# Another order of work at the turn from attention to the feed-forward part of a transformer block

## The chip, the cores and the metric

The kernel runs on one core of one Trainium2 chip. The metric is the device time of one execution, in microseconds (us). The kernel before takes 2203.07 us, the median of three executions between 2202.29 and 2204.08.

A core has five engines that work side by side, each through its own list of instructions: TensorE (PE in the profile; its weight loads are PEld), VectorE (DVE), ScalarE (ACT), GpSimd (POOL) and SyncE (SP), which here only issues DMA transfers. They wait for each other through semaphores. SBUF is the on-chip memory, PSUM the small memory into which TensorE writes sums.

## The reference

One block of a transformer on an input x of 8 batches, 512 rows and 512 columns, in float32:

```python
x = x + attention(layernorm(x))      # 16 heads, low-rank queries and keys
x = x + ffn(layernorm(x))            # 512 -> 1536 -> 512, weights rounded to fp8
layernorm(x) = (x - mean) / sqrt(var + 1e-5)
ffn(n) = (silu((n @ gate) * gs) * ((n @ up) * us)) @ down * ds
```

The change lies in the second layernorm: after the last head of a batch has been added to x, its rows are normalised, and the result is what gate and up are multiplied with.

## The kernel before, in words

The batches 0 to 7 go one after the other. Within a batch the 512 rows are four tiles of 128 rows, one row to a partition. The 16 heads of attention come first, then the feed-forward part in 12 chunks of 128 columns. Every product on TensorE is made in float16 with operands cut in two: a high half (the value rounded to float16) and a low half (what the rounding left), so that three products, or two where the weight is exact, give nearly the float32 result.

**The turn** is the stretch between the last head of a batch and the first gate products. For batches 1 to 6 it is done so:

- `add_out` (line 1956, VectorE) adds the last head to the residual rows `XR`, tile by tile, and leaves the sum of every row in `row_sum`. ScalarE follows one tile behind with `squares` (line 1496): the sum of squared deviations of each row, in `row_sq`. What it writes beside that, into `XN2`, is not used.
- VectorE makes 1/sqrt(variance) by a chain of nine small steps, each of which waits for the one before (`rsqrt`, lines 1724 to 1760; `RSQRT_OPS` is 9). Before, there are two chains: one for the tiles 0 and 1, as soon as their squares are there, and one for the tiles 2 and 3. Between the chains stands `layer_norm` (line 1788), which writes (x - mean) / deviation as float32 into `XN2` for tiles 0 and 1, and after the second chain the same for tiles 2 and 3.
- ScalarE rounds the high halves from `XN2` (`x_rows_hi`, line 1339), VectorE makes the low halves from `XN2` and the high ones (`x_rows_lo`, through `split_lo`, line 1694). The low halves of tiles 0 and 1 are put between the steps of the second chain. The high ones are in `XHL[:, 0]`, the low ones in `XHL[:, 1]`.
- SyncE issues four transposing DMAs (`turn_rows`, line 547), always in this order: high halves of tiles 0 and 1, low halves of tiles 0 and 1, high halves of 2 and 3, low halves of 2 and 3. Each waits for its two tiles. They turn rows into columns, as TensorE needs them, and end in `XTT`.
- TensorE has other work meanwhile: the last head's output, and the latent products of the next batch (`latent` in the tensor block), which end with the k latents of tile 3. Then comes `turned_gates` (lines 1156 to 1170, products at line 1142): 64 products of 128x256 for the first two chunks. The first 16 wait for the first transpose, the next 16 for the second, the next 12 for the third, the last 20 for the fourth.
- ScalarE has also the latents of the next batch to read out of PSUM (`latent`, lines 1350 and 1352), before, between and after the high halves. Its order before is: squares, latent 3, high halves 0 and 1, latents 4 and 5, high halves 2 and 3, latents 6 and 7.

All of these orders are written out by hand; nothing is planned by a scheduler. Batch 0 has a turn of its own, in which TensorE transposes the rows and one chain of nine steps serves all four tiles; batch 7 has another. The diff leaves the order of both as it is.

Of the kernel before, what the change touches and what calls it, by code (L numbers as in the profile page):

```python
# [20 lines left out]
F32 = mybir.dt.float32  # L21
# [4 lines left out]
ALU = mybir.AluOpType  # L26
ACT = mybir.ActivationFunctionType
AX_X = mybir.AxisListType.X

P = 128  # L30
B, S, H = 8, 512, 512
# [5 lines left out]
NT = S // P  # L37
# [4 lines left out]
EPS_LN = 1e-5  # L42
# [3 lines left out]
XS = 2.0**6  # L46
# [61 lines left out]
def build(nc, x, w_a, w_pe, w_nope, w_k, w_v, w_o, norm_cols, kv_norm_row, w_ffn,  # L108
# [3 lines left out]
    with ctx:  # L112
        def sb(name, shape, dt):
            return ctx.enter_context(nc.sbuf_tensor(name, shape, dt))
# [32 lines left out]
        rden_end = sb("rden_end", [P, NT], F32)  # L147
        row_sum = sb("row_sum", [P, NT], F32)
        row_sq = sb("row_sq", [P, NT], F32)


        ARENA_B = 109056
# [158 lines left out]
        def any_bank(n):  # L311
# [5 lines left out]
            "stored", "turn", "c_cols", "k_scaled", "ab_psum", "vo_psum", "w_hi", "w_lo", "ab_cp", "ab_hi", "ab_lo",  # L317
            "f_a", "f_aw", "f_b", "f_bw", "f_clip", "f_diff", "f_free",
            "ln_chain", "set_chain", "rms_chain", "k_chain",
            "ln1_chain", "x32", "xs", "xt1", "xn", "xtp", "xth", "xtl", "qkv", "ssq",  # L320
            "kvh", "kvl", "qsh", "qsl", "kt_t", "kr", "kph", "kpl",
            "qpp", "rot4", "rot", "qpeh", "qpel",
            "lat", "qap", "qah", "qal", "mxr", "shift",
# [954 lines left out]
        def _(act):  # L1278
# [55 lines left out]
            def x_rows_hi(b, t):  # L1334

                if t == 0:
                    act.wait_ge(s["ctp"], (b + 1) * N_CT)
                act.wait_ge(s["xn"], (b + 1) * NT + t + 1)
                act.activation(XHL[:, 0, t, :], XN2[:, t, :], ACT.Copy, scale=XS).then_inc(s["xth"], 1)

            def latent(a, i, setup=False):

                which, t = latents_order(setup)[i]
                n, raw = (QL, QN[:, t, :]) if which == "q" else (KL, KRAW[:, t, :])
                src = latent_banks(setup, a)[which][t]
                act.wait_ge(s["qkv"], a * (2 * NT) + (i + 1))
                if not (setup and i == 0):
                    act.wait_ge(s["ssq"], a * (2 * NT) + i)
                col = 0 if which == "q" else 1
                act.activation(JUNK[:, 0:n], src[:, 0:n], ACT.Square, scale=float(PROJ / np.sqrt(n)),  # L1350
                               accum_out=ss[:, t, col:col + 1]).then_inc(s["ssq"], 1)
                act.activation(raw, src[:, 0:QL if which == "q" else KL + DR], ACT.Copy).then_inc(s["lat"], 1)
# [156 lines left out]
            def attention(b, last, first, plain):  # L1509
                base = b * NH  # L1510
                if not first:
                    act.wait_ge(s["yo"], b * NT)
                if not plain:
                    act.wait_ge(s["t_out"], 16 * N_DUO)
                if plain:
                    probs(base, 0, True)
                    qa_hi(base + 2, 0)
                    rot_hi(b, rot_first(b))
                else:
                    probs_divided(b, 0)  # L1520
                if first:
                    rot_hi(b, N_ROT - 2)
                    probs(base + 1, 1, False)
                    rot_hi(b, N_ROT - 1)
                elif plain:
                    probs(base + 1, 1, False)
                    for n in range(rot_first(b) + 1, N_ROT):
                        rot_hi(b, n)
                else:
                    probs_divided(b, 1)  # L1530
                qa_hi(base + 3, 1)
                if not plain:
                    rot_hi(b, N_ROT_FFN)
                if first:
                    round_half(0)
                    round_rest(0)
                    for i in range(2, NH - 2):
                        head_step(i, base, i % 2, chunk=chunk_of(i), weights=True)
                elif plain:
                    for i in range(2, NH - 2):  # L1540
                        head_step(i, base, i % 2)
                        if i >= 4 and i % 2 == 0:
                            sum_hi(i // 2 - 2)
                        for t in ROWS_PLAIN.get(i, ()):
                            next_rows_hi(b, t)
                else:
                    for i in range(2, NH - 2):
                        probs_divided(b, i)
                        qa_hi(base + i + 2, i % 2)
                        if i in STG_STEPS and not last:  # L1550
                            next_rows_hi(b, STG_STEPS.index(i))
                for k in range(2):
                    i = NH - 2 + k
                    if first and k == 0:
                        output_hi(i)
                    if plain:
                        probs(base + i, k, False)
                    else:
                        probs(base + i, k, False, halves_landed(b, i), (b, i - 2))
                    if first and k == 0:  # L1560
                        output_hi(NH - 1)
                        round_half(chunk_of(i))
                        round_rest(chunk_of(i))
                    if plain and not first and k == 0:
                        sum_hi(N_DUO - 2)
                    if not last:
                        latent(b + 1, k)
                if first:
                    round_half(chunk_of(NH - 1))
                    round_rest(chunk_of(NH - 1))  # L1570
                elif plain:
                    sum_hi(N_DUO - 1)
                if last:
                    made = order_of_duo(b, N_DUO - 1)
                    context_half_hi(b, 0)
                    context_half_hi(b, 1)
                    squares(b, 0, made + 6)
                    squares(b, 1, made + 7)
                    x_hi(b + 1, (0, 1))
                    squares(b, 2, made + 11)  # L1580
                    squares(b, 3, made + 12)
                    x_hi(b + 1, (2, 3))
                    return
                latent(b + 1, 2)
                if not plain:
                    context_half_hi(b, 0, VBANK_LATE, NH - 1)
                    context_half_hi(b, 1, VBANK_LATE, NH - 1)
                for t in range(NT):
                    squares(b, t, (b * NH + NH - 1) * NT + t + 1)
                if first:  # L1590
                    for i in range(3, 2 * NT - 2):
                        latent(b + 1, i)
                    x_hi(b + 1, (0, 1))
                    latent(b + 1, 2 * NT - 2)
                    x_hi(b + 1, (2, 3))
                    latent(b + 1, 2 * NT - 1)
                    return
                latent(b + 1, 3)
                x_rows_hi(b, 0)
                x_rows_hi(b, 1)  # L1600
                latent(b + 1, 4)
                latent(b + 1, 5)
                x_rows_hi(b, 2)
                x_rows_hi(b, 3)
                latent(b + 1, 6)
                latent(b + 1, 7)

# [84 lines left out]
        def _(dve):  # L1692
# [28 lines left out]
                dve.wait_ge(s["f_clip"], c + 1)  # L1721
                dve.tensor_tensor(f_clip, f_b16[k], f_clip, ALU.subtract).then_inc(s["f_diff"], 1)

            def rsqrt(ch, v, n, eps, ops=range(RSQRT_OPS), at=0, out=None, scale=1.0, of=None, within=None):

                ve, y, t, u = rs_v[:, at:at + n], rs_y[:, at:at + n], rs_t[:, at:at + n], rs_u[:, at:at + n]
                as_v = (lambda a: a.rearrange("p (a b) -> p a b", a=v.shape[1])) if len(v.shape) == 3 else lambda a: a
# [1 line left out]

                def link(ins):  # L1730
                    ch.add(ins)
                    if within is not None and k in within:
                        within[k]()
                    ch.wait()

                for k in ops:
                    if k == 0 and of is not None:
# [23 lines left out]

            LN_N = 9 + RSQRT_OPS
            LN2_N = 1 + RSQRT_OPS
            LN3_N = 1 + 2 * RSQRT_OPS

            def norms_done(b):
                return LN_N if isinstance(b, int) and b == 0 else LN_N + LN2_N + (b - 1) * LN3_N

            assert LN_N == 18

# [25 lines left out]

            def x_rows_lo(b, t):

                dve.wait_ge(s["xth"], (b + 1) * NT + t + 1)
                split_lo(XHL[:, 1, t, :], XN2[:, t, :], XS, XHL[:, 0, t, :]).then_inc(s["xtl"], 1)  # L1800

            LN1_N = 9 + RSQRT_OPS

# [372 lines left out]
            def last_of_attention(b, first):  # L2176
# [57 lines left out]
                if first:  # L2234
# [5 lines left out]
                    layer_norm(XN2, XR)  # L2240
                    x_lo(u)
                    return
                lo, hi = row_sq[:, 0:2], row_sq[:, 2:4]
                dve.wait_ge(s["sq"], b * NT + 2)
                rsqrt(ch, lo, 2, EPS_LN, range(0, 1), of=1.0 / H ** 3)
                means()
                rsqrt(ch, lo, 2, EPS_LN, range(1, RSQRT_OPS), of=1.0 / H ** 3)
                layer_norm(XN2, XR, (0, 1))
                dve.wait_ge(s["sq"], b * NT + NT)
                rsqrt(ch, hi, 2, EPS_LN, at=2, of=1.0 / H ** 3,  # L2250
                      within={1: lambda: x_rows_lo(b, 0), 3: lambda: x_rows_lo(b, 1)})
                assert ch.n == LN3_N
                layer_norm(XN2, XR, (2, 3))
                x_rows_lo(b, 2)
                x_rows_lo(b, 3)

            def ffn(b, last, first):
                def tile_step(c):
# [399 lines left out]
```

## Time and profile before

| | |
|---|---|
| median of three executions | 2203.07 us |
| the profiled execution | 2201.61 us |
| its span | 2199.8 us |
| TensorE busy | 2170.0 us (99%) |
| VectorE busy | 1575.5 us (72%) |
| ScalarE busy | 1306.4 us (59%) |
| GpSimd busy | 1361.5 us (62%) |
| granted TensorE clock | 1.0 of full speed |

The profile is of one execution. Times in its rows are microseconds from the start of its span; a batch takes about 266 us of it. "x2" behind a row means that two instructions of one kind were joined in it; the time is then from the first one's start to the last one's end. What stands in square brackets is how long the engine sat idle before the row, and who ended that.

### The profile page before, as it was taken

The page shows a single profiled execution, that of the slowest core. Times are in us where ns is not written, and L with a number is a line of the kernel's source. Part 1 is how long each engine was busy: PE and PEld are TensorE (multiplying, and loading weights), DVE is VectorE, ACT ScalarE, POOL GpSimd, SP SyncE. Part 2 cuts the span into 40 slices and gives each one's busy share as a digit, 9 for nine tenths or more (in the row PEclk, how much of TensorE's full clock was granted, in tenths as well). Part 3 has the DMA queues.
Part 4 walks back from the last instruction along what each step waited for, and adds up shares of the span by engine and source line. Part 5 has one row for each costly group of instructions (what it writes and reads, how often), then busy time and mean ns, then how long its engine had stood idle before and what let it go on. Part 6 is the DMA issues. An engine that isn't in the chain of part 4 may idle for free.

```text
span 2199.8 us, 37599 instructions
## 1 busy us (share of the span) xinstructions
PE 2170.0 (99%) x11728; PEld 1099.1 (50%) x11728; DVE 1575.5 (72%) x3593; ACT 1306.4 (59%) x2764; POOL 1361.5 (62%) x1083
## 2 busy tenths in 40 slices
PE   7999999999999999999999999999999999999999
PEld 5444544445445564455644555445554556445554
DVE  7888786877677775777667776577766777467773
ACT  6666664555377742876428754487534875367732
POOL 4656465785378733987249772588535884368742
PEclk9999999999999999999999999999999999999999
DMA  7868436766168940788408873198632996248740
GB/s 246 192 122 149 100 72 151 154 139 151 30 127 161 167 116 19 158 161 166 99 27 164 164 152 84 46 167 159 138 80 64 165 170 125 48 99 157 152 82 20
DMA packets 759721, 271.86 MB, mean 124 GB/s; under 512 B 712656, under 2 KB 729040, under 8 KB 758480
## 3 DMA queue, kind: packets, MB, share of 16 engines
q1 hardware_dynamic: 759504, 269.35, 59.6%
q8 instruction: 90, 1.47, 0.3%
q14 instruction: 127, 1.04, 0.1%
HBM read 79.31 MB, written 14.81 MB: 43 GB/s over the span
## 4 chain that ended last, share of the span: by engine, by line
PE 89%; DVE 5%; DMA 2%; ACT 1%; POOL 1%; issue 1%; SPq 0%; ACTq 0%; DVEq 0%; POOLq 0%
PE bank L1180 12%; PE bank L961 9%; PE scores L1190 7%; PE bank L359 7%; PE bank L361 7%; PE bank L360 7%; PE scores L847 5%; PE scores L361 5%; PE scores L360 5%; PE scores L359 5%; PE bank L866 4%; PE bank L868 4%; PE bank L867 4%; PE scores L844 3%; DMA arena<-arena 2%; PE bank L1142 2%
## 5 line engine op out<-in xcount | busy, mean ns | idle before, releaser
L1926 DVE TENSOR_REDUCE mx<-scores 128x1 f32<-128x512 f32 x512 | 353.2, 690 | 61.1 <-PE scores L361 60.8
L2471 POOL TENSOR_TENSOR arena<-arena 128x1024 f16<-128x1024 f32 x168 | 354.4, 2131 | 37.0 <-ACT arena L1448 37.0
L1432 ACT ACTIVATE arena<-scores,shift 128x512 f32<-128x512 f32 x336 | 229.3, 686 | 146.8 <-DVE shift L1928 101.7
L1180 PE MATMUL bank<-arena,WFF 128*128 128x512 f16 x1296 | 292.8, 379 | 0.8 <-DVE arena L2262 0.6
L2011 DVE SCALAR_TENSOR_TENSOR arena<-bank,arena 128x512 f32<-128x512 f32 x336 | 217.0, 686 | 75.9 <-PE bank L961 74.6
L2572 POOL TENSOR_TENSOR arena<-arena 128x512 f16<-128x512 f32 x96 | 115.1, 1199 | 251.2 <-ACT arena L1618 251.2
L2384 POOL TENSOR_TENSOR arena<-arena 128x1024 f16<-128x1024 f32 x88 | 187.8, 2138 | 94.1 <-ACT arena L1422 93.6
L961 PE MATMUL bank<-WVO 128*128 128x256 f16 x1764 | 213.6, 273 | 0.2 <-DVE arena L2011 0.2
L1180 PEld LDWEIGHTS bank<-arena,WFF 128*128 128x128 f16 x1296 | 126.6, 98 | 152.8 <-DVE arena L2262 2.3
L847 PE MATMUL scores<-arena 128*128 128x512 f16 x512 | 195.4, 382 | 0.0
L961 PEld LDWEIGHTS bank<-WVO 128*128 128x128 f16 x1764 | 172.1, 98 | 46.1 <-DVE arena L2011 1.4
L359 PE MATMUL scores<-arena 128*128 128x512 f16 x512 | 194.0, 379 | 0.0
L360 PE MATMUL scores<-arena 128*128 128x512 f16 x512 | 194.0, 379 | 0.0
L361 PE MATMUL scores<-arena 128*128 128x512 f16 x512 | 194.0, 379 | 0.0
L1420 ACT ACTIVATE arena<-scores,shift 128x512 f32<-128x512 f32 x176 | 122.4, 696 | 119.6 <-DVE shift L1928 113.9
L1612 ACT ACTIVATE arena<-bank,gsc 128x512 f32<-128x512 f32 x96 | 65.6, 683 | 203.5 <-PE bank L1180 168.4
L866 PE MATMUL bank<-arena 128*128 128x512 f16 x476 | 180.4, 379 | 1.3 <-DMA arena<-arena 1.0
L868 PE MATMUL bank<-arena 128*128 128x512 f16 x476 | 180.4, 379 | 0.0
L867 PE MATMUL bank<-arena 128*128 128x512 f16 x476 | 180.4, 379 | 0.0
L1190 PE MATMUL scores<-WFF,arena 128*128 128x512 f16 x736 | 173.9, 379 | 0.0
L2459 POOL TENSOR_TENSOR arena<-arena,rden_duo 128x512 f32<-128x512 f32 x102 | 108.0, 1066 | 102.2 <-DVE rden_duo L1969 102.2
L1446 ACT ACTIVATE arena<-arena,rden_duo 128x512 f16<-128x512 f32 x234 | 166.7, 712 | 0.0
(206 smaller groups left out, 4727.8 us busy)
## 6 DMA issues: line engine op xcount, KB each, us to landing
WVO<-w_duo SPq DMA_DIRECT2D x42, 512.0 KB, 4.5
WVO<-w_duo SPq DMA_DIRECT2D x42, 384.0 KB, 3.9
arena<-arena SPq DMA_TRANSPOSE x736, 3.3
arena<-w_ffn SPq DMA_DIRECT2D x24, 384.0 KB, 3.5
arena<-x SPq DMA_DIRECT2D x8, 1024.0 KB, 5.7
out<-arena SPq DMA_DIRECT2D x32, 256.0 KB, 2.1
arena<-x SPq DMA_DIRECT2D x14, 512.0 KB, 5.8
WVO<-w_o SPq DMA_DIRECT2D x4, 1024.0 KB, 8.2
```

The source lines that it names most:

```text
L359: pe.matmul(dst, lhsT=ls(0), rhs=rs(0), start=first, stop=False)
L360: pe.matmul(dst, lhsT=ls(0), rhs=rs(1), start=False, stop=False)
L361: return pe.matmul(dst, lhsT=ls(1), rhs=rs(0), start=False, stop=last)
L847: pe.matmul(dst, lhsT=Q1[:, par, tile(t)], rhs=KA[:, :], start=False, stop=False)
L866: pe.matmul(dst[:, :], lhsT=KV[:, 0, j, :], rhs=PT[:, par, 0, :, j, :], start=(j == 0), stop=False)
L867: pe.matmul(dst[:, :], lhsT=KV[:, 1, j, :], rhs=PT[:, par, 0, :, j, :], start=False, stop=False)
L868: m = pe.matmul(dst[:, :], lhsT=KV[:, 0, j, :], rhs=PT[:, par, 1, :, j, :], start=False, stop=(j == NT - 1))
L961: r = pe.matmul(dst, lhsT=XP[j % 2][:, p, x, tile(t)], rhs=WB[:, q, w, :], start=(start and t == 0 and m == 0), stop=(m == 2), skip_group_ ...
L1180: m = pe.matmul(dst[:, :], lhsT=w[:, c, k, :], rhs=rows(p, k), start=(k == 0 and p == 0), stop=(k == NK - 1 and p == 1))
L1190: m = pe.matmul(SC[:, t, :], lhsT=FU[:, c % 4, p, tile(t)], rhs=WD[:, c, :], start=(c == 0 and p == 0), stop=(c == NF - 1 and p == 1))
L1926: dve.tensor_reduce(mx[:, t:t + 1], SC[:, t, :], AX_X, ALU.max).then_inc(s["mxr"], 1)
L2471: pool.tensor_tensor(PL[:, par, two, :], exps(i)[:, two, :], PH[:, par, two, :], ALU.subtract).then_inc(s["pl"], 1)
```

## The change

In batches 1 to 6 one chain of nine steps serves all four tiles. It starts when all four tiles have their squares. Its result carries the scale XS = 64 that the halves have. A new small instruction on VectorE makes `rs_n` = -mean times that root, with a semaphore `nb` of its own. ScalarE no longer reads `XN2`: it makes a high half from `XR` in one activation, root times x plus `rs_n`, as soon as `nb` is raised. VectorE then makes `XN2` for all four tiles and after that the four low halves. On ScalarE latent 5 moves behind the high halves of tiles 2 and 3. SyncE's and TensorE's lists stay as they are.

```diff
+        rs_n = sb("rs_n", [P, NT], F32)
...
@@ x_rows_hi (ScalarE)
-                act.wait_ge(s["xn"], (b + 1) * NT + t + 1)
-                act.activation(XHL[:, 0, t, :], XN2[:, t, :], ACT.Copy, scale=XS).then_inc(s["xth"], 1)
+                act.wait_ge(s["nb"], b)
+                act.activation(XHL[:, 0, t, :], XR[:, t, :], ACT.Identity, scale=rs_y[:, t:t + 1],
+                               bias=rs_n[:, t:t + 1]).then_inc(s["xth"], 1)
@@ attention (ScalarE)
                 x_rows_hi(b, 0)
                 x_rows_hi(b, 1)
                 latent(b + 1, 4)
-                latent(b + 1, 5)
                 x_rows_hi(b, 2)
                 x_rows_hi(b, 3)
+                latent(b + 1, 5)
                 latent(b + 1, 6)
                 latent(b + 1, 7)
@@ x_rows_lo (VectorE)
+                dve.wait_ge(s["xn"], (b + 1) * NT + t + 1)
                 dve.wait_ge(s["xth"], (b + 1) * NT + t + 1)
-                split_lo(XHL[:, 1, t, :], XN2[:, t, :], XS, XHL[:, 0, t, :]).then_inc(s["xtl"], 1)
+                split_lo(XHL[:, 1, t, :], XN2[:, t, :], 1.0, XHL[:, 0, t, :]).then_inc(s["xtl"], 1)
@@ last_of_attention (VectorE)
-                lo, hi = row_sq[:, 0:2], row_sq[:, 2:4]
-                dve.wait_ge(s["sq"], b * NT + 2)
-                rsqrt(ch, lo, 2, EPS_LN, range(0, 1), of=1.0 / H ** 3)
                 means()
-                rsqrt(ch, lo, 2, EPS_LN, range(1, RSQRT_OPS), of=1.0 / H ** 3)
-                layer_norm(XN2, XR, (0, 1))
                 dve.wait_ge(s["sq"], b * NT + NT)
-                rsqrt(ch, hi, 2, EPS_LN, at=2, of=1.0 / H ** 3,
-                      within={1: lambda: x_rows_lo(b, 0), 3: lambda: x_rows_lo(b, 1)})
-                assert ch.n == LN3_N
-                layer_norm(XN2, XR, (2, 3))
-                x_rows_lo(b, 2)
-                x_rows_lo(b, 3)
+                ch.wait()
+                rsqrt(ch, row_sq[:], NT, EPS_LN, scale=XS, of=1.0 / H ** 3)
+                dve.scalar_tensor_tensor(out=rs_n[:], in0=mv[:, :, 0], scalar=-1.0, in1=rs_y[:, 0:NT], op0=ALU.mult,
+                                         op1=ALU.mult).then_inc(s["nb"], 1)
+                assert ch.n == LN2_N
+                layer_norm(XN2, XR)
+                for t in range(NT):
+                    x_rows_lo(b, t)
```

The rest of the diff is bookkeeping: the count of chain steps per batch in `norms_done`, the semaphore's name, and the way in which `rsqrt` writes down the value it waits for, which is the same value for every chain that is left.

## Rows read from the trace of the kernel before

**Rows 1.** Page, part 1: busy us (share of the span) x instructions.
```profile
PE 2170.0 (99%) x11728; PEld 1099.1 (50%) x11728; DVE 1575.5 (72%) x3593; ACT 1306.4 (59%) x2764; POOL 1361.5 (62%) x1083
```

**Rows 2.** Timeline, gate products of batches 1, 2, 3, 4, 5, 6: start, us, engine, line.
```profile
536.35 7.29 PE L1142 MATMUL bank<-arena,WFF 128*128 128x256 f16 x64 [0.16 <-DMA arena<-arena]
801.64 7.44 PE L1142 MATMUL bank<-arena,WFF 128*128 128x256 f16 x64
1067.29 3.65 PE L1142 MATMUL bank<-arena,WFF 128*128 128x256 f16 x32 [0.19 <-DMA arena<-arena]
1071.70 3.67 PE L1142 MATMUL bank<-arena,WFF 128*128 128x256 f16 x32 [0.76 <-DMA arena<-arena]
1337.58 3.67 PE L1142 MATMUL bank<-arena,WFF 128*128 128x256 f16 x32 [0.36 <-DMA arena<-arena]
1604.95 3.67 PE L1142 MATMUL bank<-arena,WFF 128*128 128x256 f16 x32 [1.57 <-DMA arena<-arena]
1867.08 7.21 PE L1142 MATMUL bank<-arena,WFF 128*128 128x256 f16 x64 [0.16 <-DMA arena<-arena]
```

**Rows 3.** Timeline of batch 3's turn: VectorE and ScalarE.
```profile
1060.23 0.16 DVE L1738 TENSOR_SCALAR rs_v<-row_sq 128x2 f32<-128x2 f32 x1
1061.14 0.18 ACT L1496 ACTIVATION_READ_ACCUMULATOR arena<-arena,row_sum 128x1 f32 x1
1062.08 1.00 DVE L1788 TENSOR_SCALAR arena<-arena,mv,rs_y 128x512 f32<-128x512 f32 x2
1062.66 1.15 ACT L1339 ACTIVATE arena<-arena 128x512 f16<-128x512 f32 x2 [0.44 <-DVE arena L1788]
1063.72 0.47 ACT L1350 ACTIVATE arena<-scores 128x384 f16<-128x384 f32 x1
1064.55 0.28 ACT L1350 ACTIVATE arena<-scores 128x128 f16<-128x128 f32 x1
1066.35 1.15 ACT L1339 ACTIVATE arena<-arena 128x512 f16<-128x512 f32 x2 [1.21 <-DVE arena L1788]
1067.02 1.29 DVE L1694 SCALAR_TENSOR_TENSOR arena<-arena 128x512 f16<-128x512 f32 x2 [0.24 <-ACT arena L1339]
1068.49 0.34 ACT L1352 ACTIVATE arena<-scores 128x192 f32<-128x192 f32 x1
```

**Rows 4.** Timeline of batch 0's turn, VectorE: one chain for four tiles.
```profile
257.96 0.17 DVE L1738 TENSOR_SCALAR rs_v<-row_sq 128x4 f32<-128x4 f32 x1 [0.83 <-ACT arena L1496]
259.75 1.92 DVE L1788 TENSOR_SCALAR arena<-arena,mv,rs_y 128x512 f32<-128x512 f32 x4
```

**Rows 5.** Timeline, transposes of batch 3 as SyncE issues them (x4 from first, x3 from second).
```profile
1063.91 7.01 SPq L547 DMA_TRANSPOSE arena<-arena  x4
1065.27 5.65 SPq L547 DMA_TRANSPOSE arena<-arena  x3
```

**Rows 6.** Chain of waits, third transpose in batches 2, 3, 4, 5: issued, us to landing.
```profile
802.15 3.22 DMA arena<-arena
1067.60 4.06 DMA arena<-arena
1333.89 3.65 DMA arena<-arena
1599.97 4.93 DMA arena<-arena
```

**Rows 7.** DMA queues between 1067.6 and 1072 us: packets, MB, share of 16 engines.
```profile
q1 hardware_dynamic: 2089, 0.52, 91.6%
q8 instruction: 1, 0.02, 2.0%
```

**Rows 8.** Groups of ScalarE: busy us, mean ns of one, idle before.
```profile
L1446 ACT ACTIVATE arena<-arena,rden_duo 128x512 f16<-128x512 f32 x234 | 166.7, 712 | 0.0
L1339 ACT ACTIVATE arena<-arena 128x512 f16<-128x512 f32 x24 | 13.8, 622 | 9.8 <-DVE arena L1788 9.8
L1660 ACT ACT_TABLE_LOAD x1 | 1.3, 1283 | 0.7 <-PEq L2623 0.7
```

More of the change, by code:

```diff
@@ L319, in build @@
             "ln_chain", "set_chain", "rms_chain", "k_chain",
-            "ln1_chain", "x32", "xs", "xt1", "xn", "xtp", "xth", "xtl", "qkv", "ssq",
+            "ln1_chain", "x32", "xs", "xt1", "xn", "nb", "xtp", "xth", "xtl", "qkv", "ssq",
             "kvh", "kvl", "qsh", "qsl", "kt_t", "kr", "kph", "kpl",
@@ L1722, in join_chunk, with rsqrt @@
                 dve.tensor_tensor(f_clip, f_b16[k], f_clip, ALU.subtract).then_inc(s["f_diff"], 1)
-            def rsqrt(ch, v, n, eps, ops=range(RSQRT_OPS), at=0, out=None, scale=1.0, of=None, within=None):
+            def rsqrt(ch, v, n, eps, ops=range(RSQRT_OPS), at=0, out=None, scale=1.0, of=None, within=None, alone=True):
                 ve, y, t, u = rs_v[:, at:at + n], rs_y[:, at:at + n], rs_t[:, at:at + n], rs_u[:, at:at + n]
@@ L1731, in link @@
                     ch.add(ins)
+                    done = ch.n
                     if within is not None and k in within:
                         within[k]()
-                    ch.wait()
+                    if alone:
+                        dve.wait_ge(ch.sem, ch.base + done)
                 for k in ops:
@@ L1763, in _ @@
             LN2_N = 1 + RSQRT_OPS
-            LN3_N = 1 + 2 * RSQRT_OPS
             def norms_done(b):
-                return LN_N if isinstance(b, int) and b == 0 else LN_N + LN2_N + (b - 1) * LN3_N
+                return LN_N + b * LN2_N
             assert LN_N == 18
```

## The prediction, made before the changed kernel was run

> **What bounds the kernel now.** I read the page's busy times first: TensorE is busy for 2170.0 of 2199.8 us [rows 1], so a change that takes work from VectorE or ScalarE is worth nothing by itself. It counts only through what it does to the 30 us in which TensorE waits. The timeline at the first gate products, the first work that needs the rows of the turn, shows these waits [rows 2]: TensorE comes from the next batch's latents and finds the first transpose just landed or not quite (0.16 to 0.25 us idle, in batch 2 none), then works through 32 products. In batches 3, 4 and 5 it stops once more before the other 32, for 0.76, 0.36 and 1.57 us; in batches 1, 2 and 6 it does not. Then it hardly stops until the next turn, so a delay of these products goes whole into the end time. The question is when the four transposes land.
>
> The timeline of batch 3 gives the order that leads to them. I call zero the start of the first root step, 1060.23 [rows 3]. The normalised tiles 0 and 1 start at 1062.08, their high halves run from 1062.66 to 1063.81, SyncE issues the first transpose at 1063.91 and the second, being busy with the first, 1.36 us later at 1065.27 [rows 5]; it lands well before TensorE wants it. The third waits for the high halves of tiles 2 and 3 (1066.35 + 1.15 = 1067.50 [rows 3]) and is issued at 1067.60 [rows 6]. TensorE was ready for gate products at 1067.29 - 0.19 = 1067.10 [rows 2], and no edit moves that.
>
> **The change part by part.**
>
> *Later start of the chain.* It now waits for the fourth tile's squares. Their accumulator read ends at 1061.14 + 0.18 = 1061.32 [rows 3]; a step follows such an end by 0.02 (batch 0), so the chain starts at 1061.34, 1.11 after zero. This wait is covered by nothing: VectorE has only the one mean step to do meanwhile, and behind the wait stand the chain, the four normalisations and the low halves.
>
> *The chain itself.* Nine steps on four tiles are shown by batch 0: 259.75 - 257.96 = 1.79 us to the first normalisation [rows 4]. That ends it at 1063.13. The step that makes `rs_n` takes 0.17 like its neighbours, 1063.30. Nine steps of the second chain disappear, but nothing waited for VectorE after that chain except the third and fourth transpose.
>
> *High halves without `XN2`.* Before, ScalarE waited for one normalised tile, 1062.66 - 1062.08 = 0.58 after the chain [rows 3]. Now it waits for `rs_n`, 0.17 + 0.03 after it, and starts at 1063.33. So the shortcut returns 0.38 of the 1.05 that the chain lost: 0.67 later than before.
>
> *The price of the new activation.* A plain copy of 128x512 from SBUF to float16 takes 622 ns, one with a per-partition scale 712 [rows 8], so one such operand costs 90. No row has an activation with both scale and bias per partition. Below, the second one is free: 712. Above, I let it cost as much again: 802. I take the upper end, since nothing in the rows shows an operand read for nothing. Two copies take 1.15 together where one takes 0.62, an overlap of 0.09; a pair of new ones is 2 x 0.80 - 0.09 = 1.51 against 1.15, so 0.36 more (0.18 at the lower end, and none if neither operand cost anything). The Trainium skill, ScalarE: Activation LUTs, section "What ACT_TABLE_LOAD costs", says that an activation takes 186 ns plus 0.833 ns an element and that each per-partition operand adds about 93. By it the new one is an estimated 799 ns; with the second operand free it would be 706. The trace agrees for none and for one, and no row shows two.
>
> *First transpose.* 0.67 + 0.36 = 1.03 later: issued at 1064.94. TensorE starts its gate products 3.38 us after this issue (1067.29 - 1063.91), so at 1068.32 where it was 1067.29, and it idles 1.22 us in place of 0.19.
>
> *Second transpose.* VectorE starts to normalise at 1063.24 (it does not wait for `rs_n` to be written), takes 1.92 for four tiles [rows 4], and has the low halves of tiles 0 and 1 another 1.29 later [rows 3], at 1066.4. SyncE, free at 1066.30, issues at 1066.5, 1.2 later than before. Landing 3.2 after that, at 1069.7, it is ahead of its use: the first 16 products take half of 3.65, so it is wanted at 1068.32 + 1.83 = 1070.15. Cover 0.45 us; it had 0.7.
>
> *Third and fourth transpose.* Latent 4 on ScalarE takes 0.83 (1063.72 to 1064.55 [rows 3]), so the high halves of tiles 2 and 3 end near 1064.85 + 0.75 + 1.51 = 1067.1, before SyncE is through with the second transpose at 1066.5 + 1.36 = 1067.86. The third is then issued at 1067.86 instead of 1067.60: queue-bound now, 0.26 later. Wanted at 1068.32 + 3.65 = 1071.97, it may take 4.1 us and cost nothing. The fourth follows at 1069.2 with its low halves long made. So the second stop of TensorE mostly disappears: it is not saved but eaten by the later start.
>
> *Latent 5 behind the high halves, and its two successors,* end at 1069.2 in place of 1068.83 [rows 3]. They feed the next batch's keys on GpSimd, whose results TensorE wants a whole feed-forward part later; that work hides it, and with it gone the price would be 0.4 a turn.
>
> *Sum over the six turns.* The end of the 64 products moves by 1.03 less the old second stop, plus a new one where the third transpose is still late. Batches 1 and 6: +1.03 each. Batch 2: its 64 products took 7.44 where batch 6 took 7.21 [rows 2], so 0.2 is absorbed: +0.8. Batch 3: 1.03 - 0.76 = +0.27. Batch 4: 1.03 - 0.36 = +0.67. Batch 5: 1.03 - 1.57 = -0.54, but if its third transpose again takes 4.93 [rows 6] TensorE stops 0.8 for it: +0.26. Together +4.1, or +3.3 if no transpose is slow any more. Against the profiled 2201.61 that is 2205.7; the median of the runs lies 1.46 above the profiled execution, and I add the same there: 2207.1 us, 0.18% more than 2203.07. A measurement of this kernel can tell about 0.2% (4.4 us) from no change, so this counts as no change, barely.
>
> **The rivals.**
>
> *Cheaper activations and no slow transposes.* The third transpose is slow (3.65 to 4.93 against 3.22) where a packet of instructions, 16 KB on q8, falls among the transposes [rows 6, 7]. If the new order escapes these packets and the second operand is free, the six terms are 3.3 - 6 x 0.18 = +2.2, 2205.3; with both operands free +1.1, 2204.2. For it: the packets hit only three turns of six. Against it: TensorE's list, which they feed, is untouched, and it comes 1 us later together with the transposes.
>
> *A new wait: the second transpose.* This is the case on the other side. It has only 0.45 us of cover. If the packet now falls on it instead of the third and it lands 4.06 to 4.93 after issue, TensorE stops 0.4 to 1.3 us in the middle of the first 32 products; it decides from a landing of 3.65 on. In the three turns that had a packet this adds 1.2 to 3.8 us to the +3.3: +4.5 to +7.1, middle 5.8, 2208.9. For it: the second is now in flight at 1066.5 to 1069.7, and the slow third of batch 3 was in flight from 1067.60. Against it: batch 2 had its transposes at the same places and none was slow.
>
> *A table load.* Identity is a function that the kernel before does not use. If it had to be loaded, every turn would pay 1.283 us [rows 8] before the high halves and again at the next other function: +8 at the least, 2215. The trace runs copy, square, exp and tanh with one load in all. By the Trainium skill, ScalarE: Activation LUTs, section "Table sets: the hidden batching unit", cheap functions, identity among them, are in every set, so no load would come; no run so far shows it.
>
> *Faster by 0.2%.* It needs a gain of 4.4 us where the old second stops are 2.7 in all [rows 2] and the first transpose is later in every turn. I see no way; the instructions saved on VectorE lie beside TensorE's work.
>
> **How the numbers follow.** Forecast 0.47, cheap case 0.20, new wait 0.26, table load 0.03, faster 0.03, something else 0.01. The forecast's own range is 2205.8 to 2208.3. The overall range, 2204.1 to 2209.4, takes in the cheap case and most of the new wait. The 0.2% bound is 2207.5: two thirds of the forecast and all of the cheap case lie below it, nearly all of the new wait above. Faster 0.03, same 0.56, slower 0.41.
>
> **What would show each step.** In the turn of batch 3 of the changed kernel: one chain whose first step starts 1.1 us after the last add's accumulator read; the high halves' activation at 0.80 us (0.71 would give back 0.2 a turn); no second ACT_TABLE_LOAD; TensorE idle for about 1.2 us before the gate products in all six turns, and little or nothing between the two groups of 32. The forecast is wrong if the idle time before the gate products stays near 0.2, if a stop stands before the second 16 products, or if a feed-forward part takes another time than before.

## The result: 2208.2 us, 0.24% more than before

The changed kernel takes 2208.21 us (median of 17 runs, 2205.8 to 2210.09), the kernel before 2202.99 us in the same number of runs. The ratio is 1.0024, 95% interval 1.0018 to 1.0030. The forecast was 2207.1 in a range of 2204.1 to 2209.4. It called this no change, barely. The measured 5.2 us lie just above the bound of 4.4, so the time was forecast and the class was not: it is slower, by an interval that is clear of zero. Whether it is slower by more than the bound is not settled, since the interval (4.0 to 6.6 us) holds 4.4.

The profiled execution took 2208.59 us, its span is 2206.8. TensorE's busy time has not moved [rows 1], VectorE has 5.1 us less and ScalarE 3.6 us more:

```profile
PE 2170.1 (98%) x11728; PEld 1098.6 (50%) x11728; DVE 1570.4 (71%) x3545; ACT 1310.0 (59%) x2764; POOL 1361.5 (62%) x1083
```

So the lost time is waiting of TensorE. The timeline of the changed kernel at the gate products, batches 1 to 6 in order, answers to [rows 2]; the bracket is the idle time before the row:

```profile
538.36 7.15 PE L1143 MATMUL bank<-arena,WFF 128*128 128x256 f16 x64 [1.63 <-DMA arena<-arena]
805.05 7.15 PE L1143 MATMUL bank<-arena,WFF 128*128 128x256 f16 x64 [1.31 <-DMA arena<-arena]
1071.58 3.65 PE L1143 MATMUL bank<-arena,WFF 128*128 128x256 f16 x32 [1.35 <-DMA arena<-arena]
1075.70 3.67 PE L1143 MATMUL bank<-arena,WFF 128*128 128x256 f16 x32 [0.48 <-DMA arena<-arena]
1338.69 3.65 PE L1143 MATMUL bank<-arena,WFF 128*128 128x256 f16 x32 [1.30 <-DMA arena<-arena]
1342.90 3.67 PE L1143 MATMUL bank<-arena,WFF 128*128 128x256 f16 x32 [0.55 <-DMA arena<-arena]
1606.71 4.96 PE L1143 MATMUL bank<-arena,WFF 128*128 128x256 f16 x44 [1.35 <-DMA arena<-arena]
1612.16 2.36 PE L1143 MATMUL bank<-arena,WFF 128*128 128x256 f16 x20 [0.49 <-DMA arena<-arena]
1874.49 7.15 PE L1143 MATMUL bank<-arena,WFF 128*128 128x256 f16 x64 [1.34 <-DMA arena<-arena]
```

The first stop is 1.3 us in every turn, where it was 0.2 or nothing. The second stop is still there in batches 3 to 5, though smaller in two of them. Measured from the last add (the accumulator read of its row sum, "zero" of the prediction) to the end of the 64 products, the six turns have become longer by 1.33, 1.03, 0.87, 1.31, 0.02 and 1.11 us, 5.7 together. That is the measured change of the medians, within its uncertainty. The two profiled spans differ by 7.0 us, however; the other 1.3 lie outside the turns (0.5 before the last add of batch 1, 1.1 in the stretches from one turn to the next, 0.4 less behind the last turn), and nothing here assigns them to the change.

The timeline of batch 3's turn in the changed kernel, VectorE, ScalarE and SyncE, answers to [rows 3 to 5]; zero is 1063.36:

```profile
1063.36 0.08 DVE L1960 DVE_READ_ACCUMULATOR arena<-scores,rden,arena 128x1 f32 x1
1064.26 0.19 ACT L1498 ACTIVATION_READ_ACCUMULATOR arena<-arena,row_sum 128x1 f32 x1
1064.48 0.17 DVE L1742 TENSOR_SCALAR rs_v<-row_sq 128x4 f32<-128x4 f32 x1 [0.84 <-ACT arena L1498]
1066.27 0.16 DVE L2251 SCALAR_TENSOR_TENSOR rs_n<-mv,rs_y 128x4 f32<-128x4 f32 x1
1066.35 1.91 DVE L1791 TENSOR_SCALAR arena<-arena,mv,rs_y 128x512 f32<-128x512 f32 x4
1066.52 1.52 ACT L1340 ACTIVATE arena<-arena,rs_n,rs_y 128x512 f16<-128x512 f32 x2 [1.18 <-DVE rs_n L2251]
1068.13 5.58 SPq L548 DMA_TRANSPOSE arena<-arena  x4
1068.17 1.28 DVE L1696 SCALAR_TENSOR_TENSOR arena<-arena 128x512 f16<-128x512 f32 x2
1068.78 1.51 ACT L1340 ACTIVATE arena<-arena,rs_n,rs_y 128x512 f16<-128x512 f32 x2
```

The reader sees the forecast chain: VectorE idle for 0.84 us until the fourth tile's squares are there, nine steps, `rs_n`, the pair of activations in 1.52 us, the first transpose 4.77 us after zero where it was 3.68. All four transposes now stand back to back on SyncE's queue (5.58 us, four of 1.4).

### The profile page after: what moved, and what is told of

It reads as the page before. It is cut to its first block, busy times and chain, and to the rows that moved or that the text cites. A ratio compares the mean times of both kernels' runs of the same rounds, so it can differ in the third digit from the quotient of the medians.

```text
span 2206.8 us, 37560 instructions
## 1 busy us (share of the span) xinstructions
PE 2170.1 (98%) x11728; PEld 1098.6 (50%) x11728; DVE 1570.4 (71%) x3545; ACT 1310.0 (59%) x2764; POOL 1361.5 (62%) x1083
## 4 chain that ended last, share of the span: by engine, by line
PE 84%; DVE 5%; ACT 3%; DMA 3%; SPq 2%; POOL 2%; issue 1%; ACTq 0%; DVEq 0%; POOLq 0%
PE bank L1181 12%; PE bank L962 9%; PE scores L1191 7%; PE bank L360 6%; PE bank L362 6%; PE bank L361 6%; PE scores L848 5%; PE scores L360 5%; PE scores L362 5%; PE scores L361 5%; PE bank L867 4%; PE bank L869 4%; PE bank L868 4%; PE scores L845 3%; DMA arena<-arena 2%; PE bank L1143 2%
```

## The experiments

The turn sum below is that measure of each kernel's profile, zero to the end of the 64 products, summed over the six turns, less the same sum of the kernel before (88.8 us). It comes from one profile of each kernel; the time comes from 6 to 11 runs. Times are medians; the kernel before, run beside them, had 2202.9 in the first four and 2202.6 in the last four.

**Only the late start.** Everything is as before the change, except that the first chain waits for all four squares:

```diff
-                dve.wait_ge(s["sq"], b * NT + 2)
+                dve.wait_ge(s["sq"], b * NT + NT)
                 rsqrt(ch, lo, 2, EPS_LN, range(0, 1), of=1.0 / H ** 3)
```

> The kernel before with one wait changed: its first chain of root steps (tiles 0 and 1) waits for the squares of all four tiles instead of the first two; both chains, the order and ScalarE's copies stay. Theory (the late start of the chain is what costs): the first transpose is issued 1.1 us later in each of six turns, TensorE idles about 1.3 us before the gate products instead of 0.2, and the third transpose, whose chain follows the first, is 1.1 later too, so the second stops of batches 3 to 5 remain: about +1.1 x 6 = +6.6 us over the kernel before (5 to 8). Rival (TensorE's second stops, made by slow transposes, are what differs between the two kernels): the first stop is absorbed by them and the time is within 3 us of before.

Measured: 2209.97 us, ratio 1.0032 (1.0020 to 1.0044); turn sum +7.2. The timeline of this kernel at the gate products of batches 3 and 5:

```profile
1071.07 3.65 PE L1142 MATMUL bank<-arena,WFF 128*128 128x256 f16 x32 [1.32 <-DMA arena<-arena]
1075.30 3.67 PE L1142 MATMUL bank<-arena,WFF 128*128 128x256 f16 x32 [0.58 <-DMA arena<-arena]
...
1606.09 3.65 PE L1142 MATMUL bank<-arena,WFF 128*128 128x256 f16 x32 [1.33 <-DMA arena<-arena]
1611.34 3.67 PE L1142 MATMUL bank<-arena,WFF 128*128 128x256 f16 x32 [1.60 <-DMA arena<-arena]
```

One wait moved by one argument makes the changed kernel's first stop, 1.3 us, and costs as much as the whole change does or a little more: the intervals of the two times overlap, the turn sum is 1.5 higher, mostly in batch 5, whose second stop stays at 1.60. The rival, that the old second stops would swallow it, is out.

**The one chain without the direct reading.** The changed kernel with ScalarE's old copy:

```diff
-                act.activation(XHL[:, 0, t, :], XR[:, t, :], ACT.Identity, scale=rs_y[:, t:t + 1],
-                               bias=rs_n[:, t:t + 1]).then_inc(s["xth"], 1)
+                act.wait_ge(s["xn"], (b + 1) * NT + t + 1)
+                act.activation(XHL[:, 0, t, :], XN2[:, t, :], ACT.Copy).then_inc(s["xth"], 1)
```

> The changed kernel, but ScalarE makes the high halves as before the change: a plain copy of the normalised tile XN2, which it waits for. Theory: the direct reading saves 0.38 us of waiting and pays 0.36 for its two per-partition operands (806 ns against 622), so undoing it moves the first transpose by less than 0.1 us and the time by less than 1 us from the changed kernel (2207.5 to 2209). Rival (the direct reading is the part that costs, for ScalarE's time): 2 us or more faster than the changed kernel. Other rival (it is the part that helps): 2 us or more slower.

Measured: 2208.62 us, ratio 1.0028 (1.0017 to 1.0039); turn sum +5.2 against the changed kernel's +5.7. In batches 2 to 6 the first transpose is issued 4.8 us after zero, as in the changed kernel. Within the noise the direct reading is worth nothing here, in either direction. In this run's profile the pair of copies starts 3.57 after zero and takes 1.15; in the changed kernel the pair starts 3.16 after zero and takes 1.52:

```profile
1065.17 1.15 ACT L1341 ACTIVATE arena<-arena 128x512 f16<-128x512 f32 x2 [1.59 <-DVE arena L1791]
```

**The direct reading without the one chain.** The changed kernel with two chains again, each followed by its two `rs_n`:

```diff
-                rsqrt(ch, row_sq[:], NT, EPS_LN, scale=XS, of=1.0 / H ** 3)
...
+                lo, hi = row_sq[:, 0:2], row_sq[:, 2:4]
...
+                dve.wait_ge(s["sq"], b * NT + 2)
+                rsqrt(ch, lo, 2, EPS_LN, range(0, 1), of=1.0 / H ** 3, scale=XS)
+                means()
+                rsqrt(ch, lo, 2, EPS_LN, range(1, RSQRT_OPS), of=1.0 / H ** 3, scale=XS)
+                shifts(slice(0, 2))
+                layer_norm(XN2, XR, (0, 1))
+                dve.wait_ge(s["sq"], b * NT + NT)
+                rsqrt(ch, hi, 2, EPS_LN, at=2, of=1.0 / H ** 3, scale=XS,
+                      within={1: lambda: x_rows_lo(b, 0), 3: lambda: x_rows_lo(b, 1)})
+                shifts(slice(2, 4))
...
+                layer_norm(XN2, XR, (2, 3))
+                x_rows_lo(b, 2)
+                x_rows_lo(b, 3)
```

> The changed kernel with its one chain undone: two chains of two tiles as before, each followed by its two rs_n values, and ScalarE reads the sums directly. Theory (only the one chain costs): the first chain starts at the last add again, the first transpose is issued 3.6 to 3.7 us after it as in the kernel before, TensorE idles about 0.2 before the gate products, and the time is that of the kernel before within 1.5 us (2202 to 2204.5). Rival (the direct reading costs): it stays near the changed kernel, 2206 or more.

Measured: 2203.62 us, ratio 1.0004 (0.9995 to 1.0013); turn sum +0.6. The timeline at the gate products of batch 3 has the small first stop again:

```profile
1068.23 3.65 PE L1143 MATMUL bank<-arena,WFF 128*128 128x256 f16 x32 [0.16 <-DMA arena<-arena]
```

In batch 4 the turn is 0.6 longer than before; there and in batch 3 an instruction packet (see below) stretched SyncE's issue of the third transpose from 1.23 to 2.4 and 2.2 us.

Together the three runs settle the cause: the one chain costs, because it has to wait for the fourth tile. What is left of the change without it (the direct reading, latent 5 behind the high halves) costs 0.7 us, in an interval of -1.1 to +2.9.

**The activation without its operands.** The changed kernel with `ACT.Copy, scale=XS` in place of the activation with scale and bias per row. The high halves are then not normalised; the low halves, made as `XN2` less the high ones, take up the rest.

> The changed kernel with the two per-partition operands left out of ScalarE's activation: a plain copy of the sums, scaled by 64, so the high halves are not normalised and the output is not the reference's; all waits stay. Theory: the pair of activations takes 1.15 us instead of 1.52, the first transpose is issued 0.37 us earlier, and the six turns give back 6 x 0.37 = 2.2 us, less where a slow transpose takes it: 1 to 2.5 us faster than the changed kernel. Rival (the second transpose, with the low halves, becomes the limit at once): the first 16 gate products start earlier but stop before the next 16, and under 0.7 us is gained.

Measured: 2207.83 us, ratio 1.0023 (1.0014 to 1.0032), 0.4 less than the changed kernel, with intervals that overlap; turn sum +4.4, 1.3 less. The first transpose was issued 4.42 after zero in batch 3, 0.36 sooner as expected. But in batches 3 and 4 the second one was now the limit. The timeline of batch 3, with a stop after 16 products that neither kernel had:

```profile
1072.00 1.91 PE L1143 MATMUL bank<-arena,WFF 128*128 128x256 f16 x16 [0.75 <-ACT arena L1353]
1075.07 5.42 PE L1143 MATMUL bank<-arena,WFF 128*128 128x256 f16 x48 [1.16 <-DMA arena<-arena]
```

The theory's 1 to 2.5 us holds in the turns of the profile, the rival's "under 0.7" in the time; the run does not decide between them. Its second transposes landed 4.4 and 4.6 us after issue in those batches and 3.2 to 3.3 in the other four. That is the new wait that the prediction held as a rival, brought about by another edit: the packets came 2.6 us after the issue of these two transposes.

**What makes a transpose slow.** The changed kernel and the kernel before, each with 128 instructions more at the head of TensorE's list:

```diff
             pe.wait_ge(s["ld_id"], 16)
+            pad = ident[:].bitcast(F16)
+            for _ in range(64):
+                pe.matmul(BT[:, 0:8], lhsT=pad[:, 0:P], rhs=pad[:, 0:8], start=True, stop=True)
             for t in range(NT):
                 x_transposes(0, t, XN)
```

> The changed kernel with 64 small products put ahead of TensorE's list, where it waits for the first rows anyway (their sums are not used): 128 instructions more, half of the 256 that one 16 KB packet holds. Nothing else of the turn changes. Theory (a transpose is slow when the packet with TensorE's next instructions is fetched while it is in flight): the packets of batches 3, 4 and 5, now 9.6 to 11.5 us after the last add, move out of the transposes, so their third and fourth transposes land in 3.1 to 3.4 us and the second stops (0.48, 0.55, 0.49) vanish; the packet of batch 1 moves into the gate products (11 to 13 after the last add). First stops stay at 1.3 to 1.6: 0.5 to 2 us faster than the changed kernel. Rival (the transposes are slow because the four are issued back to back): the same transposes of batches 3 to 5 stay at 4.1 to 4.7 us.

> The kernel before with the same 64 products ahead of TensorE's list. Theory (packets): the third transposes of batches 3, 4 and 5, which took 4.1, 3.6 and 4.9 us, take 3.1 to 3.3, and the second stops (0.76, 0.36, 1.57) vanish: up to 2.7 us faster than before, less what packets cost at other places. Rival (they are slow for a reason that lies in the turn): the three stops stay where they are.

Measured for the changed kernel with the shift: 2208.84 us, ratio 1.0032 (1.0020 to 1.0044), against its own 2208.21; turn sum +4.2, 1.4 less. For the kernel before with the shift: 2202.56, ratio 1.0000 (0.9990 to 1.0009); turn sum -1.7. So neither became faster, though the turns did. The four transposes of batch 3, landing times in the kernel before and then in the shifted one:

```profile
L547 SPq DMA_TRANSPOSE arena<-arena x4: 1234/1262/1975, 1063.9 to 1068.9; - x4
DMA to landing us min/median/max: 3.1/3.6/4.1
```

```profile
L547 SPq DMA_TRANSPOSE arena<-arena x4: 1234/1256/1269, 1067.7 to 1072.8; - x4
DMA to landing us min/median/max: 3.1/3.2/3.3
```

And the timeline at the gate products of batches 1, 3 and 5 in the kernel before with the shift, and of batch 3 in the changed kernel with it:

```profile
537.98 3.65 PE L1142 MATMUL bank<-arena,WFF 128*128 128x256 f16 x32 [0.29 <-DMA arena<-arena]
542.84 3.67 PE L1142 MATMUL bank<-arena,WFF 128*128 128x256 f16 x32 [1.21 <-DMA arena<-arena]
...
1071.15 7.22 PE L1142 MATMUL bank<-arena,WFF 128*128 128x256 f16 x64 [0.20 <-DMA arena<-arena]
...
1601.99 7.29 PE L1142 MATMUL bank<-arena,WFF 128*128 128x256 f16 x64 [0.16 <-DMA arena<-arena]
...
1073.99 7.15 PE L1143 MATMUL bank<-arena,WFF 128*128 128x256 f16 x64 [1.35 <-DMA arena<-arena]
```

The second stops of batches 3 to 5 are gone in both kernels and one has come up in batch 1, into whose turn the packet moved (in the kernel before with the shift it comes 10.1 us after zero; in batch 3 it came 8.2 after zero without the shift, and with it one comes 0.3 before zero and the next at 15.2). The turn itself, its order and its transposes are the same. So back-to-back issue is not what makes them slow, nor are the weight transfers on the same queue (in the changed kernel's batch 3 SyncE issues the first of them 10.5 after zero, with the shift 10.4); the packet of TensorE's instructions is.

The time did not fall with the turns. In the kernel before, the padding took 1.87 us in which TensorE waited anyway, yet the last add of batch 1 came at 530.79 instead of 529.29. Most of that is the same effect at another place. In the last head of batch 1 a packet comes at 523.3, 2.0 us after a transpose is issued at 521.24; that one lands after 4.50 us where it took 3.23, and the products behind it wait. The timeline at these products, the kernel before and then with the shift:

```profile
524.28 1.48 PE L881 MATMUL bank<-arena 128*128 128x256 f16 x12 [0.32 <-DMA arena<-arena]
```

```profile
525.78 1.49 PE L881 MATMUL bank<-arena 128*128 128x256 f16 x12 [1.60 <-DMA arena<-arena]
```

All three kernels with the shift have this stop (1.59 to 1.64), and in the seven without it the stop is 0.17 to 0.32. The rest lies in short waits of batch 0, which were not followed up; without the shift the last add of batch 1 comes anywhere from 528.1 to 531.1 in the profiles.

**The high halves made by VectorE.** Two chains, and behind each VectorE writes the high halves itself, in float16, straight from the sums. ScalarE makes `XN2`, which only the low halves need:

```diff
+                def rows_hi(tiles):
+                    pair = slice(tiles[0], tiles[1] + 1)
+                    dve.scalar_tensor_tensor(out=rs_n[:, pair], in0=mv[:, pair, 0], scalar=-1.0, in1=rs_y[:, pair],
+                                             op0=ALU.mult, op1=ALU.mult).then_inc(s["nb"], 1)
+                    for t in tiles:
+                        dve.tensor_scalar(XHL[:, 0, t, :], XR[:, t, :], mv[:, t, 0:1], rs_y[:, t:t + 1], ALU.subtract,
+                                          ALU.mult).then_inc(s["xth"], 1)
...
@@ ScalarE
+                act.activation(XN2[:, t, :], XR[:, t, :], ACT.Identity, scale=rs_y[:, t:t + 1],
+                               bias=rs_n[:, t:t + 1]).then_inc(s["xn"], 1)
```

> Two chains as before the change, but VectorE writes the high halves itself in float16 straight from the sums, right behind each chain, and ScalarE makes the float32 rows XN2 (its activation with both operands) that only the low halves need. Theory (the first transpose must be issued 3.5 us or less after the last add, then the third one decides): first transpose at 3.0 to 3.1 instead of 3.67, no stop before the gate products; third at 6.9 instead of 7.4; the second stops get smaller by 0.5: 1 to 2.5 us faster than the kernel before. Rival (VectorE pays for the float16 writing, or the low halves wait for ScalarE): the first transpose gains, but the second or third is later than before and the time is within 1 us of before or above it.

> The kernel of e7 with the 64 products ahead of TensorE's list. Theory: both gains add up, since one removes the first stop and the other the second: no stop over 0.2 us in five or six of the turns, 2.5 to 4 us faster than the kernel before. Rival (packets moved here hit other transposes, in other turns or among the heads): no faster than e7.

Measured: 2200.16 us, ratio 0.9986 (0.9977 to 0.9995), turn sum -2.8; with the shift 2200.50, ratio 0.9990 (0.9981 to 0.9999), turn sum -4.3. The timeline of batch 3's turn in the version without the shift, zero 1059.76:

```profile
1061.67 1.00 DVE L2255 TENSOR_SCALAR arena<-arena,mv,rs_y 128x512 f16<-128x512 f32 x2
1061.79 1.52 ACT L1340 ACTIVATE arena<-arena,rs_n,rs_y 128x512 f32<-128x512 f32 x2
1062.77 7.44 SPq L548 DMA_TRANSPOSE arena<-arena  x4
...
1066.46 5.20 PE L1143 MATMUL bank<-arena,WFF 128*128 128x256 f16 x44
1072.06 2.36 PE L1143 MATMUL bank<-arena,WFF 128*128 128x256 f16 x20 [0.40 <-DMA arena<-arena]
```

The first transpose goes out 3.01 after zero, TensorE has no first stop in any turn, and the medians are 2.4 us apart. The gate products of batch 3 begin 6.70 after zero where they began 7.06. The last latent product before them starts 6.62 after zero in both, so the old first stop was 0.36 us, not the 0.19 in its bracket: the profile models the ends of products, and a short stop comes out too small. That is why more is gained than the brackets promise. The stop of 0.40 before the last 20 products is a packet too, 0.6 us after the issue of the third transpose: SyncE needed 2.37 us for that issue instead of 1.23, so that the fourth went out late. With the shift five of six turns have no stop at all, but the stop in batch 1's last head is there (1.59 instead of 0.18), with other waits before it, and the last add of batch 1 comes at 533.26 instead of 529.35. So the sum of both that the theory expected did not come. The rival was right on the time, and for 1.4 of these 3.9 us its reason is seen.

## Why the prediction came out as it did

- **Late start of the chain:** 1.11 us forecast; the first step started 1.12 after zero (1064.48). Shown to be the cause by the first experiment.
- **The chain and `rs_n`:** forecast to end 3.07 after zero, measured 1066.43, the same. The one chain of batch 0 was a good model.
- **Price of the activation:** 802 ns forecast from two times the step between 622 and 712 [rows 8]; the changed kernel's group has 806. From the figures of the Trainium skill, ScalarE: Activation LUTs, section "What ACT_TABLE_LOAD costs", the estimate for two operands was 799; the trace now agrees.
- **Table load:** none was added (one in all, of 1283 ns, as before), so that rival fell. The Trainium skill, ScalarE: Activation LUTs, section "Table sets: the hidden batching unit", has identity in every table set, by which no second load was due; the trace agrees in so far as it shows one load in all.
- **First transpose:** 1.03 later forecast, 1.1 measured in five turns and 1.3 in batch 1 (not pursued); TensorE idle 1.22 forecast, 1.30 to 1.35 measured in five turns and 1.63 in batch 1. The transposes that met no packet are a little slower to land, 3.1 to 3.4 where they took 3.0 to 3.3 before.
- **Second transpose:** issued 6.19 after zero in batch 3 (6.27 forecast), never waited for in the changed kernel. The new wait did not come.
- **Latent 5 behind the high halves:** the last of the latents was forecast to be read out 0.4 later; in batch 3 it was 0.1 (8.73 after zero, 8.60 before), and GpSimd began with it 0.1 later. No wait of TensorE came of it.
- **The term that was mis-sized** is the second stop: "the second stop of TensorE mostly disappears: it is not saved but eaten by the later start". I gave the third transposes of batches 3 and 4 their old landing times, 4.06 and 3.65, though I had noted that TensorE's list, and the packet with it, would come 1 us later "together with the transposes". By my own sum the third transpose was only 0.26 later, so the packet had to fall later in its flight. It did: it came 1.8 and 1.5 us later after zero, the third transposes 0.3, and both took 4.7 us to land. The stops of 0.48 and 0.55 came in place of zero, and with the longer first stops the six terms summed to 5.7 instead of 4.1. Batch 5 went the other way: the packet missed its third transpose, hit the fourth, and the turn grew by 0.02 instead of 0.26.

The number alone would not have told the forecast from its nearest rival: 2208.2 is 1.1 above the forecast and 0.7 below the middle of the new wait, 2208.9. The profile does, since no turn stops after 16 products. That the time came within 1.1 us is in part luck, as the terms of the turns missed by 1.6 in sum. And the chances of the classes do not follow from the cases: two thirds of 0.47 and all of 0.20 are 0.51 for no change, not 0.56.

The kernel is slower because the chain of four tiles starts 1.1 us later, and this is shown. The stops of half a microsecond in batches 3 and 4 come from where an instruction packet falls: with the packet moved they are gone.

## What to carry to other kernels

Where work is cut in two so that the first part can leave early, joining the parts saves instructions on an engine with time to spare and delays the part on which the bound engine waits; count from the last input that the joined chain needs. Reading an input directly gains nothing where the operands of the direct form cost as much as the wait that it saves; the same rounding, done by the engine that has just made the factors, did gain. And transfers that the bound engine awaits at a fixed place in its list should be read in every repetition, not in one: they can be slow in some for a reason that lies in the list itself. A gain from moving such a packet is worth little until all other places of the list are looked at: here it only moved the stops.

## What the runs showed of the hardware that was not expected

A transposing DMA between SBUF and SBUF (two tiles, 256 KB) lands 3.0 to 3.4 us after issue. When a 16 KB packet of instructions on q8 came while it was in flight, it mostly took longer. In the kernel before: 4.93 with a packet 2.9 us after issue, 4.30 at 1.6, 4.06 and 3.65 at 0.8, 3.88 and 3.43 with a packet that began 0.5 and 0.6 before the issue. In the changed kernel: 4.63 at 2.5, 4.66 at 2.3, 4.68 at 2.0, 4.12 at 0.9, 4.13 at 0.7. It is no fixed price. The first transpose of batch 2 in the kernel before had a packet 0.3 us after issue and landed in 3.04; there SyncE's issue took 1.71 us instead of 1.26. In the version with the halves by VectorE two second transposes had a packet 2.5 and 2.6 us after issue and landed in 3.1 and 3.0, and why these were spared is open.

The DMA queues of the changed kernel while its slow third transpose of batch 3 was in flight answer to [rows 7] (the share adds up the times of all packets, so it can pass 100%):

```profile
q1 hardware_dynamic: 2700, 0.68, 118.9%
q8 instruction: 1, 0.02, 1.4%
```

The same queue in one microsecond, from 10.64 us after zero, in the changed kernel, where the packet had come 0.7 us before, and then in the changed kernel with the shift, where none came:

```profile
q1 hardware_dynamic: 27, 0.01, 20.0%
```

```profile
q1 hardware_dynamic: 768, 0.19, 103.4%
```

So the transposes were not slowed evenly: behind the packet everything on q1 all but stopped for about a microsecond, transposes and the weight transfer beside them.

The place of the packet follows TensorE's list and not the clock: 128 instructions ahead of everything moved it in all turns at once. They are about half of what one packet brings (11728 products and as many weight loads came in 90 packets on q8, 261 to each).

One more coincidence is in the record and was not tested. In the run with ScalarE's old copy, an 8 KB instruction packet on q14 came 2.6 us after the issue of the second transpose in batches 2 to 6. These landed in 3.6 to 3.9 us; that of batch 1, without such a packet, in 3.2.
